# First half of the intra product issued directly behind the inter product instead of behind the V projection

## The reference, cut to what matters

```python
xn = layernorm(x)
q, k, v = (heads(xn @ W.T + b) for W, b in ((Wq, bq), (Wk, bk), (Wv, bv)))
q, k = softmax(exp(beta) * q), softmax(exp(beta) * k)      # over the 8 channels of a head
kv  = cumsum(einsum('zsD,zsd->zsDd', k, v), axis=1)        # over the tokens
num = einsum('zsD,zsDd->zsd', q, kv)
den = sum(q * cumsum(k, axis=1), -1)
att = (num / den) @ Wo.T + bo
ffn = fp8(xn) @ (weight_fp8 * weight_scale).T + bias
out = x + att + ffn
```

## Time and profile before

| | |
|---|---|
| median of 3 runs | 1186.12 us |
| profiled execution | 1187.5 us, of which 1185.7 us are the span of its instructions |
| TensorE busy | 1115.6 us (94%), mean granted clock 0.982 |
| VectorE, ScalarE, GpSimd busy | 967.9 us (82%), 899.3 us (76%), 463.6 us (39%) |
| matmul records | 24098 |

### The profile page before, as it was taken

The page is one execution under the profiler, slowest core; times in us unless marked ns, Lnnn a source line. Parts: engine busy times, 40 slices in busy tenths (PEclk is TensorE's granted clock), DMA queues, the critical chain, the costliest instruction groups (busy, mean ns, idle before and its releaser), DMA issues.

```text
span 1185.7 us, 57406 instructions
## 1 busy us (share of the span) xinstructions
PE 1115.6 (94%) x24098; PEld 627.9 (53%) x24098; DVE 967.9 (82%) x1968; ACT 899.3 (76%) x1933; POOL 463.6 (39%) x717
## 2 busy tenths in 40 slices
PE   1458999999999999999999999999999999999996
PEld 1224555555555555555555555555555555555553
DVE  4648888888888888888888888888888888888883
ACT  0356787888878787878888888878887878787873
POOL 3133434443433444444434443443434443434420
PEclk9689999999999999999999999999999999999999
DMA  8312434544554455445445554454333343333331
GB/s 242 27 43 69 93 87 91 87 97 87 81 94 91 87 84 97 92 82 87 95 88 86 92 95 85 81 98 93 85 83 94 88 89 86 97 87 86 73 76 48
DMA packets 156468, 104.38 MB, mean 88 GB/s; under 512 B 111968, under 2 KB 128480, under 8 KB 156256
## 3 DMA queue, kind: packets, MB, share of 16 engines
q1 hardware_dynamic: 155536, 99.76, 41.1%
q10 hardware_dynamic: 720, 1.31, 0.3%
HBM read 40.20 MB, written 16.78 MB: 48 GB/s over the span
## 4 chain that ended last, share of the span: by engine, by line
PE 91%; issue 4%; DVE 2%; DMA 2%; POOL 1%; SPq 0%; ACT 0%; POOLq 0%; DVEq 0%
PE s_ps L941 11%; PE a_ps L1045 7%; PE vo_ps L907 5%; PE k_ps L1001 5%; PE k_ps L907 5%; PE k_ps L918 5%; PE k_ps L922 5%; PE k_ps L920 5%; PE vo_ps L911 5%; PE vo_ps L909 5%; PE q_ps L909 5%; PE q_ps L911 5%; PE k_ps L911 5%; PE k_ps L909 5%; PE q_ps L907 5%; PE a_ps L1030 4%
## 5 line engine op out<-in xcount | busy, mean ns | idle before, releaser
L496 ACT ACTIVATE st_pairs<-st_run 32x144 f32<-32x144 f32 x1008 | 331.0, 328 | 11.9
L422 POOL TENSOR_TENSOR w_own<-vp,cst 128x576 f32<-128x576 f32 x126 | 141.9, 1147 | 314.0 <-DVE vp L754 314.0
L556 ACT ACTIVATE q_heads<-qT,cst 128x512 f32<-128x512 f32 x256 | 164.1, 711 | 4.9 <-DVE qT L770 3.8
L698 DVE TENSOR_TENSOR att<-s_ps,cst 128x512 f32<-128x512 f32 x256 | 163.5, 680 | 0.3 <-PE s_ps L941 0.3
L941 PE MATMUL s_ps<-q_heads,w_own 64*64 64x128 f32 x4096 | 141.6, 275 | 1.3 <-DVE att L698 1.3
L409 POOL TENSOR_TENSOR y_sum<-y,y_magic 128x512 f32<-128x512 f32 x64 | 81.6, 1274 | 151.6 <-DVE y_magic L656 151.6
L941 PEld LDWEIGHTS s_ps<-q_heads,w_own 64*64 64x64 f32 x4096 | 110.6, 132 | 55.2 <-issue 55.0
L538 ACT ACTIVATE w_own<-kT,cst 128x512 f32<-128x512 f32 x128 | 85.5, 715 | 61.3 <-DVE kT L738 61.3
L402 POOL TENSOR_TENSOR x_split<-xn,x_split 128x512 f16<-128x512 f32 x64 | 74.6, 1165 | 137.6 <-ACT x_split L479 130.4
L479 ACT ACTIVATE x_split<-xn 128x512 f16<-128x512 f32 x64 | 40.3, 630 | 99.2 <-DVE xn L645 99.2
L907 PE MATMUL k_ps<-w_hi,xT 128*128 128x512 f16 x256 | 99.0, 387 | 17.1 <-DMA xT<-x_split 12.3
(11 more groups left out here) (144 smaller groups left out, 2272.6 us busy)
## 6 DMA issues: line engine op xcount, KB each, us to landing
v_groups<-vp SPq DMA_DIRECT2D x512, 36.0 KB, 3.3
x_in<-L_attn_x SPq DMA_DIRECT2D x64, 256.0 KB
x_res<-L_attn_x SPq DMA_DIRECT2D x64, 256.0 KB
out<-o_sb SPq DMA_DIRECT2D x64, 256.0 KB
w_own<-L_attn_Wk SPq DMA_DIRECT2D x1, 1024.0 KB, 12.7
w_own<-L_attn_Wq SPq DMA_DIRECT2D x1, 1024.0 KB, 14.7
w_own<-L_attn_Wv SPq DMA_DIRECT2D x1, 1024.0 KB, 16.5
att<-L_ffn_weight_fp SPq DMA_DIRECT2D x1, 1024.0 KB, 18.2
```

The source lines that it names most:

```text
L422: last = gp.tensor_tensor(v_pairs[:, c].rearrange("p h w -> p (h w)"), vp[:, t.parity].rearrange("p h w -> p (h w)"), pair_mask[:, c:c + 1 ...
L496: last = sc.activation(st_pairs[TOK * b:TOK * (b + 1), to, u::J, :, b % SP, :], st_run[TOK * u:TOK * (u + 1), b // SP, :, b % SP, :, :], A ...
L556: last = sc.activation(q_heads[:, i.parity, :, j, :], qT[:, i.parity, :, :], ACT.Copy, scale=head_mask[:, j:j + 1])
L698: v.tensor_tensor(att[:, c % 2, 4 * (c // 2):4 * (c // 2) + 4, :, :] .rearrange("p g j s -> p (g j) s"), s_ps[:, DM * (c % 2):DM * (c % 2 ...
```

## The change

In TensorE's body the call `intra(t, 0)` moves from behind V to between inter and V. `intra(t, 1)` stays behind V. Each call carries its own waits. No instruction is added or removed.

```diff
                 if t.exists():
                     inter(t, i.exists())
+                    intra(t, 0)
                 if i.exists():
                     values(i, fold)
                 if t.exists():
-                    intra(t, 0)
                     intra(t, 1)
```

## The result

The changed kernel takes 1199.55 us (median of 5 runs, 1199.23 to 1199.87) against 1186.84 us for the kernel before, timed beside it: ratio 1.0106 (95% interval 1.0094 to 1.0117), so slower. Its profiled execution took 1199.28 us, the one before 1187.5: +11.8 us. The forecast was +11.9. By the medians of runs timed side by side it is +12.7 us, and the forecast of 1198.0 us, which started from a median of 1186.1, is 1.5 us low.

A forecast was written before the change was run, and what follows sets the result against it. TensorE, never waiting in the steady stretch, was taken as the bound; 0.23 + 0.13 - 0.16 = +0.20 us over 62 steps, +12.4, less 0.5 in body 1, gave +11.9: 1198.0 us, range 1192 to 1210.

The forecast's parts named there:

- Inter to V, 0.16 gone: TensorE's gap from inter's last start to V's first, 0.16 us a step, disappears in the new order.
- Inter to intra, 0.23 new: New gap from inter to intra's first half, 0.23 us a step, read from body 64, where no V stands between.
- The bound of 0.15: Cheaper exit from inter, read from state to transpose: 0.15 us, making a step +0.12 and 62 steps +7.4 us.
- Intra to V, 0.13 new: New gap from intra's first half to V, 0.13 us a step, taken from intra to K.
- V to intra and intra to K unchanged: Gaps around intra's second half stay: 0.30 us from V to intra, 0.13 from intra to K.
- The junction, taken as nothing: Splitting intra removes its middle junction, 0.01 us; two short blocks may differ from one long; counted as nothing.
- the rival without a drain: Inter runs on into intra at one record's pace; sum -3.7 us, including perhaps 2 us of rare pauses; 1182.4 us, chance 0.06.
- Body 1, -0.5: In body 1 intra's first half hides in V's 1.25 us wait for the folded bias: -0.5 us, or 0.
- Body 64, nothing: The last body has no V, so its order stays and nothing is added.
- The cover: Work released by V comes 0.54 us later but stays hidden: GpSimd slack 1.76 to 1.2, VectorE's wait used up, transfers cost nothing.
- A pause in the feed at each step: Inter with half of intra starves for instructions each step, costing 0.39 us a step; +23.7 us, 1209.8 us, chance 0.12.
- VectorE's delay: Rival: VectorE's 0.1 us lateness reaches TensorE each step through K's maxima and masked scores; +6 us, 1204 us, chance 0.08.

The follow-up runs named there:

- e1: Changed kernel with intra's waits for the transfers moved ahead of inter and the first half's wait for att dropped; 1200.4 us, ratio 1.0111.
- e3: e2 with the waits for the transfers moved ahead of inter as in e1; 1216.83 us, ratio 1.0231.
- e5: e1 with 64 instructions that only count a semaphore put ahead of the first body; 1195.44 us, ratio 1.007.
- e9: e5 with inter's matmuls on all 128 rows instead of 64, so it computes something else; 1210.61 us (one run).
- e2: Changed kernel with both halves of intra directly behind inter and V behind them; 1232.21 us, ratio 1.0383.
- e8: e7 with 16 instead of 112 counting instructions at the start; 1356.4 us (one run).
- e7: e3 with three extra counting instructions a body, 112 at the start, and VectorE's normalise_attention ahead of scale_values; 1199.35 us, ratio 1.0113.
- e6: e2 with 204 instructions that only count a semaphore added in the setup; 1194.31 us, ratio 1.0065.
- e11: Kernel with V ahead of inter and whole intra, transfer waits ahead, three extra counting instructions a body and 173 in the setup; 1192.11 us, ratio 1.0041.
- e12: e11 with V kept behind inter and intra in body 1 alone, and 153 instead of 173 counting instructions in the setup; 1185.73 us, ratio 0.999.

## Why the prediction was right

The step (17.28 forecast, 17.296) and the mechanism (TensorE never idle, more changes of block) held. That the total agrees to 0.1 us in the profiled executions (+11.9 forecast, +11.8) is luck: terms of 0.3 to 1.7 us that the sum had left out or taken as nothing cancel each other, and by the medians it is off by 0.8 us. By its own steps:

1. *Inter to V, 0.16 gone*: as forecast.
2. *Inter to intra, 0.23 new*: 0.227. Of the two readings of it, waits and change of shape, both are in: 0.07 waits (e1, e3, e5) and 0.15 shape (e9). The bound of 0.15 was thus the price of the change without its waits. The reason given, that nothing long hides five waits behind a dense block, fits: taken ahead of inter, behind the output product, they cost nothing (0.309 us into inter with and without them).
3. *Intra to V, 0.13 new*: 0.127.
4. *V to intra and intra to K unchanged*: 0.309 and 0.127.
5. *The junction, taken as nothing*: this term was mis-sized. Two halves take 2 x 0.573 us from first to last start, the whole 1.120, so +0.026 a step, though one record's pace went with the junction. 61 steps x 0.025 = 1.5 us. It didn't show in the sum since something opposite was left out: the rare stops, 2.5 us in the 61 steps before, 1.9 of it in intra, and 0.8 after (sums of the steps less 61 medians: 1043.95 - 1041.45 and 1055.88 - 1055.06). The prediction had named them, as "perhaps 2 us", but only for the rival without a drain.
6. *Body 1, -0.5*: from its inter to the next 18.92 us instead of 19.45, so -0.54. V starts at 96.44 and not at "about 95.9": the setup ahead of the first inter took 0.49 us longer (94.30 against 93.81). Nothing of the change lies there. The traces show where it arises: the K projection ahead of it starts 0.26 us later (79.45 against 79.19), and all its twelve matmuls are 0.43 us apart, at the lower level of the granted clock (0.50), where before the last four intervals were 0.22. TensorE's waits for VectorE between there and inter take back most of that, 1.72 us before and 0.70 after. Why the clock rose later stays open.
7. *Body 64, nothing*: its inter starts at 1181.48, 11.78 after that of before. That is the sum: 0.49 setup, -0.54 body 1, +11.93 for 61 steps, -0.09 for body 63. The prediction had +0.20 for body 63. There the kernel before loses about 0.3 us in the scores' second half, at the same place 192 modulo 256, and the changed kernel doesn't.

*The cover* was as counted: GpSimd 1.22 us of slack (1.2 forecast), VectorE's 0.55 us used up, the transfers in time.

*The rivals.* A pause in the feed at each step did not come with this change, and the reason against it, that 64 + 64 records are fewer than the old 128, is too weak as it stands: with their loads inter and half of intra are 256 records, exactly one block, and inter with the whole intra 384. The latter stops for 2 us where a border lies late in it (e2, e8). The 0.19 us of the last intra, which the rival priced its pause with, isn't the feed but the short pause described under e7. The joining without a drain is excluded by 0.227 and, for this pair of shapes, by e5's 0.153. VectorE's delay was not handed on: `normalise_attention` starts 0.11 us behind K in both kernels.

What a step's 0.22 consists of, in all: 0.15 shape and 0.07 waits at inter to intra, +0.13 intra to V, -0.16 inter to V, +0.03 for two short blocks.

## What to carry to other kernels

When TensorE is busy all the time, moving a block costs what its borders cost: read them from last start to next start for each pair of shapes, and count how many of each pair the new order has. A block of short matmuls moved between two others is an island more, and the semaphore waits at its head, free here behind 128x512 matmuls, cost 0.07 us behind a dense block. Before a dense run of short matmuls is made longer, look at where it lies in the stream of instructions: a stop with nothing but issue named, at a place that moves evenly from one pass of the loop to the next, is the feed of instructions; the instruction queue's packet that ends shortly before TensorE goes on confirms it.

## What the runs showed of the hardware that I had not expected

- **Blocks of 256 instructions.** The stops stand at one place modulo 256 of TensorE's stream, in the kernel before, e2 and e8 alike. A block's packet takes 0.9 to 1.9 us, and from its start to TensorE's going on it is 2.2 to 3.4 us in the 121 stops. No packet started while TensorE was more than 299 places ahead of the block, and 300 places of these dense matmuls and loads run in some 1.3 to 1.5 us (an estimate from 0.54 us for 64 records of intra with their loads and 0.66 for inter's 64). So a dense run as long as inter and intra together can't hide a border late in it. With V's twelve long matmuls in between, as in the kernel before, the border in intra costs at most 0.47 us, in six bodies. Many packets start later than that: for e1's last stop only at 1180.31, when TensorE already stood (from 1179.97), though the 256 places before had taken 5.1 us. The 3.5 us a block in the expectation of e5 fit e2 and not this one. What sets a packet's start stays open. The place alone moved one program from 1199 to 1356 us.
- **A stop costs more than itself.** In e8 TensorE's granted clock falls after some of them:

```profile
136.00:140.00 4.00, 2.07 (x24) 0.96 (x24) 1.73 (x6) 3.93 (x11) 0.00 (x0) 0.86 0.26 47
...
139.00:143.00 4.00, 4.00 (x13) 1.41 (x12) 0.99 (x3) 1.58 (x5) 0.00 (x0) 0.59 0.27 93
```

  It had stood still for 1.95 us until 137.93; from 138.9 to 142.3 the 128x512 matmuls start 0.43 us apart instead of 0.22, the lower of the two levels (1.2 GHz), 8 intervals, so 1.7 us more. The bodies of e2 and e8 with steps of 21 us beside those of 19 are those in which V runs like this.
- **The price of a change of shape**, from last start to next start: 0.15 us from 64*32 to 128*32, 0.13 from 128*32 to 128*128, 0.16 from 64*32 to 128*128, each against 0.01 for a record's pace; 0.31 from 128*128 to either, against the 0.22 of the long matmuls' own pace, so 0.09; nothing between equal shapes (e9, and V to K in e2).
- **A short pause late in a long dense run**: 0.11 to 0.21 us, at records 100 to 112 of intra when inter's 64 stand directly ahead (body 64 of the kernel before, e2, e3, e6, e7, e11, e12), in some bodies missing or earlier. It isn't at the borders of 256, and what it is stays open.
